# Attention over 32 images: the two half-empty key tiles of an image pair become one, and GpSimd pre-adds twelve tiles instead of nine

## The reference, cut to what matters

```python
g = clip(bn1(conv1x1(l)), 0, 6)                  # 64 channels
f = einsum('niab,nicd->nabcd', theta, theta)     # theta = first 32 channels
f = softmax(f.reshape(n, h*w, h, w), axis=1)     # over the first pixel index
f = softmax(f.reshape(n, h*w, h*w), axis=2)      # over the second pixel index
out = einsum('nabcd,nicd->niab', f, g) / h * w
out = bn2(depthwise_conv3x3(out)) + l
```

## Time and profile before

| | |
|---|---|
| median of three runs | 5523.3 us (5523.17 to 5526.93) |
| the profiled execution | 5524.6 us |
| its span | 5522.8 us |
| granted TensorE clock, mean | 0.988 |
| frames | 32, after 790 us of layer 0 |

### The profile page before, as it was taken

How to read it: one execution, slowest core, us unless ns; L and a number is a source line. 1 busy time by engine, 2 the same in 40 slices (tenths; PEclk the granted TensorE clock), 3 DMA queues, 4 the chain that set the end, 5 groups by cost and what they waited for, 6 DMA issues and landing times.

```text
span 5522.8 us, 92847 instructions
## 1 busy us (share of the span) xinstructions
PE 5347.5 (97%) x34434; PEld 2656.0 (48%) x34434; DVE 4534.5 (82%) x9093; ACT 5218.8 (94%) x3077; POOL 3992.9 (72%) x1715
## 2 busy tenths in 40 slices
PE   8999969999999999999999999999999999999996
PEld 3444434455454444444444444555544444444442
DVE  7888867888888888888888888888888888888886
ACT  7888859999999999999999999999999999999995
POOL 5666624878777777777777777887877777777775
PEclk9999979999999999999999999999999999999998
DMA  7778851222222222222222222222222222222211
GB/s 148 164 160 161 162 101 33 56 48 46 60 60 60 60 60 60 60 60 60 59 54 59 57 54 50 57 55 48 49 60 60 60 60 60 60 60 60 60 37 36
DMA packets 225087, 382.64 MB, mean 69 GB/s; under 512 B 155837, under 2 KB 173438, under 8 KB 214398
## 3 DMA queue, kind: packets, MB, share of 16 engines
q1 hardware_dynamic: 224638, 376.69, 32.8%
HBM read 260.16 MB, written 103.56 MB: 66 GB/s over the span
## 4 chain that ended last, share of the span: by engine, by line
PE 79%; issue 3%; DVE 2%; ACT 1%; DMA 0%; SPq 0%; POOL 0%; DVEq 0%; POOLq 0%
PE at_AV L924 40%; PE at_S L894 23%; PE at_AV L929 14%; PE at_AV L920 2%; DVE at_ring L803 1%; ACT at_ring L748 1%; ACT at_ring L754 1%; DVE at_OUTB L834 0%; DMA at_YT<-yd 0%; DVE at_RZ L820 0%; DMA rzd<-at_ZC 0%; DMA at_ZB<-rzd 0%; SPq L648 0%; SPq L612 0%; DVE at_CIN L830 0%
## 5 line engine op out<-in xcount | busy, mean ns | idle before, releaser
L803 DVE TENSOR_SCALAR_CACHE_REDUCE at_ring<-at_S 128x1176 f32<-128x1176 f32 (+1 forms) x2400 | 2952.7, 1242 | 323.8 <-PE at_S L894 296.5
L748 ACT ACTIVATE at_ring<-at_ring,at_NM 128x3136 f32<-128x3136 f32 (+1 forms) x800 | 2324.4, 2905 | 102.5 <-DVE at_NM L812 98.8
L712 POOL TENSOR_TENSOR at_ZP<-at_ZP,at_ring 128x1568 f32<-128x1568 f32 x512 | 1827.8, 3609 | 747.3 <-ACT at_ring L754 719.9
L924 PE MATMUL at_AV<-at_ring,at_GT 128*64 128x392 f32 x12800 | 2316.3, 501 | 8.9 <-issue 8.9
L754 ACT ACTIVATE at_ring<-at_ring,at_RZ 128x3136 f32<-128x3136 f32 (+1 forms) x800 | 2319.8, 2900 | 0.0
L894 PE MATMUL at_S<-at_THM,at_THS 128*128 128x392 f32 x6400 | 1512.2, 365 | 96.1 <-DVE at_ring L803 52.7
L894 PEld LDWEIGHTS at_S<-at_THM,at_THS 128*128 128x128 f32 x6400 | 1058.8, 187 | 799.8 <-DVE at_ring L803 505.0
L924 PEld LDWEIGHTS at_AV<-at_ring,at_GT 128*64 128x64 f32 x12800 | 837.5, 136 | 1146.5 <-issue 1109.1
L725 POOL TENSOR_TENSOR at_OUTB<-at_OUTB,at_ZB 128x1568 f32<-128x1568 f32 x248 | 887.2, 3578 | 18.1
L929 PE MATMUL at_AV<-at_ring,at_ones 128*32 128x392 f32 x8192 | 756.8, 498 | 0.0
L858 DVE TENSOR_TENSOR at_ACC<-at_AV,at_ACC 128x392 f32<-128x392 f32 x768 | 433.4, 564 | 257.2 <-PE at_AV L924 253.2
(11 more groups left out here) (64 smaller groups left out, 2385.8 us busy)
## 6 DMA issues: line engine op xcount, KB each, us to landing
l_X<-in_x SPq DMA_DIRECT2D x128, 392.0 KB, 7.4
at_THM<-hld SPq DMA_DIRECT2D x128, 392.0 KB, 8.3
at_CIN<-att SPq DMA_DIRECT2D x64, 406.0 KB, 7.6
at_ZB<-rzd SPq DMA_DIRECT2D x64, 406.0 KB, 4.9
at_THS<-hld SPq DMA_DIRECT2D x128, 200.0 KB, 4.9
yd<-l_YO SPq DMA_DIRECT2D x128, 196.0 KB, 5.5
att<-at_ACC SPq DMA_DIRECT2D x256, 98.0 KB
at_OUTB<-yd SPq DMA_DIRECT2D x64, 392.0 KB, 8.8
```

What stands on the lines that cost most here:

```text
L712: e.tensor_tensor(z, z, v, ALU.add).then_inc(g_add, 1)
L748: e.activation(v, v, ACT.Exp, bias=NM[0:k, i:i + 1], accum_out=ZS[0:k, i:i + 1]).then_inc(a_p1, 1)
L803: e.tensor_scalar(ring[0:r, s % RING, QC * a_:QC * b].rearrange("p (b w) -> p b w", w=QC), PS[0:r, k % 2, 0:b - a_, 0:QC], 1.0, None, ALU. ...
L924: ins = e.matmul(dst[64 * j:64 * j + 64, 0:QC], GT[fl.n % 2][0:r, t, :], ring[0:r, slot, q:q + QC], start=(t == GROUPS[fl.i][0]), stop=(t ...
```

## The change

- The 64 keys that are left over of image 2p and those of image 2p+1 share one tile: a pair of images takes 49 slots (`PAIR`) instead of 50. Image 2p has slots 0 to 24, image 2p+1 slots 24 to 48; slot 24 is the shared one, the last tile of the first image and the first (t = 0) of the second. `THL` holds the 64 keys of each image in its own half of 128 columns, zeros in the other half; for the shared slot each block of 392 columns takes two matmuls (one per image) that accumulate. `GT` and `ones` have zeros in the other image's half.
- `POOL_OF` becomes (2, 2, 2, 2, 2, 2, 0); in group 0 tiles 1 and 2 are taken, so the pooled tiles are 1, 2, 4, 5, 8, 9, 12, 13, 16, 17, 19, 20.
- The costs that `plan` uses for ScalarE change from 2910 and 2900 to 2810 and 2893 ns; shared score pieces cost double.
- SyncE gets the loads `thl`; the due slots of `thm`, `ths` follow the new numbering. Six more memsets stand ahead of the attention.

```diff
-KEYS = [128] * 24 + [64]
+HALF_KEYS = 24
+PAIR = 2 * NT - 1
-POOL_OF = (1, 2, 2, 2, 1, 1, 0)
-POOLED = [t for r, m in zip(GROUPS, POOL_OF) for t in r[:m]]
+POOL_OF = (2, 2, 2, 2, 2, 2, 0)
+POOLED = [t for g, (r, m) in enumerate(zip(GROUPS, POOL_OF)) for t in (r[:m] if g else r[1:1 + m])]
+def base(n):
+    return PAIR * (n // 2) + (NT - 1) * (n % 2)
+def keys_of(n, t):
+    return t if n % 2 == 0 else t - 1 if t else HALF_KEYS
+def tiles_of(s):
+    p, r = divmod(s, PAIR)
+    return ([(2 * p, r)] if r < NT else []) + ([(2 * p + 1, r - NT + 1)] if r >= NT - 1 else [])
...
-    total = NT * n_img
+    total = PAIR * n_img // 2
...
-            ta = t_a + (2910 if n_a % 2 or n_a == 0 else 2900)
+            ta = t_a + (2810 if n_a % 2 or n_a == 0 else 2893)
...
+                tp = t_s + 178 * (b - a) * len(tiles_of(n_s // NP)) + turn
...
-        THS = sb("THS", [128, HW], F32R)
+        THS = sb("THS", [128, 2 * HALF], F32R)
+        THL = sb("THL", [128, 2, 128], F32R)
...
+            def thl(n):
+                if n >= 2:
+                    e.wait_ge(pe_s, NP * (PAIR * (n // 2 - 1) + NT))
+                i = n % 2
+                for blk in range(4):
+                    e.dma_start(THL[32 * blk:32 * blk + 32, i, 64 * i:64 * i + 64].bitcast(F32),
+                                hld[n, blk // 2, :, 2 * HALF:]).then_inc(s_thl, 16)
...
-                todo.append((f - NT + 0.2 if n >= 1 else -9, thm, (n,)))
-                todo.append((f - NT + 13 if n >= 1 else -8, ths, (n, 0)))
-                todo.append((f + 0.1 if n >= 1 else -7, ths, (n, 1)))
+                todo.append((f - NT + 1.2 if n >= 1 else -9, thm, (n,)))
+                todo.append((f - NT + 14 if n >= 1 else -8, ths, (n, 0)))
+                todo.append((f - NT + 15 if n >= 2 else -6.5, thl, (n,)))
+                todo.append((f + 1.1 if n >= 1 else -7, ths, (n, 1)))
...
                 for j in range(a_, b):
-                    ins = e.matmul(PS[0:r, k % 2, j - a_, 0:QC], THS[:, 128 * t:128 * t + r],
-                                   THM[n % 2][:, QC * j:QC * j + QC], start=True, stop=True)
+                    for i, (n, t) in enumerate(of):
+                        q = 128 * keys_of(n, t)
+                        own = THS[:, q:q + 128] if len(of) == 1 else THL[:, i, :]
+                        ins = e.matmul(PS[:, k % 2, j - a_, 0:QC], own, THM[n % 2][:, QC * j:QC * j + QC],
+                                       start=(i == 0), stop=(i == len(of) - 1))
```

More of the change, by code:

```diff
@@ L71, in plan @@
         for b, r in enumerate(BATCHES):
-            f = NT * (n - 1) + 8 + 4 * b
+            f = base(n) - NT + 8 + 4 * b
             pre.append(Fill("g", n, b, 0, f if n else -1, f + 3 if n else -1))
         for g, r in enumerate(GROUPS):
-            first = NT * n + r[-1]
+            first = base(n) + r[-1]
             main += [Fill("o", n, g, p, first, 0) for p in range(4)]
             main += [Fill("z", n, g, i, first, 0) for i in range(2)]
-    adds = [(NT * n + t, h) for n in range(n_img) for t in POOLED for h in range(2)]
+    adds = [(n, t, h) for n in range(n_img) for t in POOLED for h in range(2)]
     conv = [(n, step) for n in range(n_img - 1) for step in range(20)]
@@ L138, in plan @@
             if s >= RING:
[L139 to L142, removed]
+                for m, u in tiles_of(s - RING):
+                    free = max(free, group_end.get((m, group_of(u)), inf) + LAT)
+                    if u in POOLED:
+                        free = max(free, end_add.get((m, u, 1), inf) + LAT)
             cv.append((max(td, end_s.get(n_m, inf) + LAT, free), 2, "M"))
@@ L154, in plan @@
         if adds:
-            s, h = adds[0]
-            n, t = divmod(s, NT)
+            n, t, h = adds[0]
             free = -inf
@@ L159, in plan @@
                 free = summed.get((n - 1, h), inf) + LAT
-            cg.append((max(tg, end_p2.get(s, inf) + LAT, free), 0, "add"))
+            cg.append((max(tg, end_p2.get(base(n) + t, inf) + LAT, free), 0, "add"))
         if conv:
@@ L228, in plan @@
             if what == "add":
-                s, h = adds.pop(0)
-                n, t_ = divmod(s, NT)
+                n, t_, h = adds.pop(0)
                 tg = end_add[n, t_, h] = t + (1700 if t_ == POOLED[0] else 3600)
-                pool.append(("add", s, h))
+                pool.append(("add", (n, t_), h))
             else:
@@ L543, in attention @@
         RZ = sb("RZ", [128, 4])
-        ones = sb("ones", [128, 32])
+        ones = sb("ones", [128, 3, 32])
         WG = sb("WG", [65, C])
@@ L607, in ths @@
             def ths(n, h):
-                lo, hi = (0, HALF) if h == 0 else (HALF, HW)
+                lo, hi = (0, HALF) if h == 0 else (HALF, 2 * HALF)
                 if n >= 1:
-                    e.wait_ge(pe_s, NP * (NT * (n - 1) + (12 if h == 0 else NT)))
+                    e.wait_ge(pe_s, NP * (base(n - 1) + (n - 1) % 2 + (12 if h == 0 else 24)))
                 for blk in range(4):
@@ L686, in _ @@
         def _(e):
-            for t in (ones,):
-                e.memset(t[:, :], 1.0).then_inc(g_ms, 1)
+            e.memset(ones[:, 0, :], 1.0).then_inc(g_ms, 1)
+            e.memset(ones[:, 1:3, :], 0.0).then_inc(g_ms, 1)
+            e.wait_ge(g_ms, 2)
+            for i in range(2):
+                used, rest = (slice(64 * i, 64 * i + 64), slice(64 - 64 * i, 128 - 64 * i))
+                e.memset(ones[used, 1 + i, :], 1.0).then_inc(g_ms, 1)
+                e.memset(GT[i][rest, HALF_KEYS, :], 0.0).then_inc(g_ms, 1)
+                e.wait_ge(g_ms, 4 + 2 * i)
+            e.memset(THL[:, :, :].bitcast(F32), 0.0).then_inc(g_ms, 1)
             e.memset(CIN[:, :, :], 0.0).then_inc(g_ms, 1)
@@ L699, in _, with add @@
             T3 = ZB[:, 1:29, :]
-            def add(s, h):
-                n, t = divmod(s, NT)
+            def add(n, t, h):
+                s = base(n) + t
                 v = ring[:, s % RING, HW // 2 * h:HW // 2 * (h + 1)]
@@ L731, in _ @@
                 if what == "add":
-                    add(n, i)
+                    add(*n, i)
                 else:
@@ L844, in evacuate @@
                     r = BATCHES[fl.i]
-                    full = [t for t in r if KEYS[t] == 128]
-                    spans = [(128, full[0], len(full))] + [(KEYS[t], t, 1) for t in r if KEYS[t] != 128]
+                    full = [t for t in r if t != HALF_KEYS]
+                    h = 64 * (fl.n % 2)
+                    spans = [(slice(0, 128), full[0], len(full))] + [(slice(h, h + 64), HALF_KEYS, 1)] * (HALF_KEYS in r)
                     for p, t0, m in spans:
                         o = t0 - r[0]
-                        v = src[0:p, 64 * o:64 * (o + m)].rearrange("p (t c) -> p t c", c=64)
-                        ins = e.tensor_scalar(GT[fl.n % 2][0:p, t0:t0 + m, :], v, 0.0, 6.0, ALU.max, ALU.min)
+                        v = src[p, 64 * o:64 * (o + m)].rearrange("p (t c) -> p t c", c=64)
+                        ins = e.tensor_scalar(GT[fl.n % 2][p, t0:t0 + m, :], v, 0.0, 6.0, ALU.max, ALU.min)
                 elif fl.kind == "o":
@@ L882, in scores @@
                 s, c = divmod(k, NP)
[L883 to L889, removed]
+                of = tiles_of(s)
+                for n, t in of:
+                    if t == 0 and c == 0:
+                        e.wait_ge(s_thm[n % 2], 64 * (n // 2 + 1))
+                    if keys_of(n, t) in (0, 12) and c == 0:
+                        e.wait_ge(s_ths[keys_of(n, t) // 12], 64 * (n + 1))
+                if len(of) == 2 and c == 0:
+                    e.wait_ge(s_thl, 128 * (of[0][0] // 2 + 1))
                 if k >= 2:
@@ L913, in unit @@
                     else:
-                        e.wait_ge(a_p2, NT * fl.n + GROUPS[fl.i][-1] + 1)
+                        e.wait_ge(a_p2, base(fl.n) + GROUPS[fl.i][-1] + 1)
                         e.wait_ge(v_ev, index["g", fl.n, 3, 0] + 1)
-                o = t - BATCHES[fl.i][0] if fl.kind == "g" else 0
-                slot = (NT * fl.n + t) % RING
+                slot = (base(fl.n) + t) % RING
+                part = 0 if t == SUM or keys_of(fl.n, t) != HALF_KEYS else 1 + fl.n % 2
                 for _, j in fl.units[i]:
                     if fl.kind == "g":
-                        ins = e.matmul(dst[0:r, 64 * o:64 * o + 64], YT[(4 * fl.n + fl.i) % 2][:, 128 * o:128 * o + r],
+                        o = t - BATCHES[fl.i][0]
+                        a_, b = (128 * o, 128 * o + 128) if t != HALF_KEYS else (128 * o - 64 * (fl.n % 2), 128 * o + 64)
+                        ins = e.matmul(dst[0:b - a_, 64 * o:64 * o + 64], YT[(4 * fl.n + fl.i) % 2][:, a_:b],
                                        WG[:, :], start=True, stop=True)
@@ L923, in unit @@
                         q = QC * (2 * fl.j + j)
-                        ins = e.matmul(dst[64 * j:64 * j + 64, 0:QC], GT[fl.n % 2][0:r, t, :], ring[0:r, slot, q:q + QC],
```

(6 more changed lines are left out.)

49 lines of the change are left out of this document (24 added, 25 removed).

## The result

The changed kernel takes 5719.7 us (median of four runs, 5712.66 to 5723.8) against 5523.7: a ratio of 1.035, 95% interval 1.033 to 1.037. It is 196 us slower; I had forecast 92.

The account below looks back on a forecast made before the run. TensorE bounds by a small margin, ScalarE next. Frame 139.4 + 1.3 + 7.0 + 1.3 = 149.0 us against 145.8; thirty such frames +96, two others -10, start and tail +2: +88, giving 5615 us, range 5395 to 5760.

Parts of the forecast that it names:

- parts 1 and 2: Per frame, ScalarE needs 139.4 us (2.9 less) and TensorE 140.0 (4.2 less); with 1.3 of ScalarE waiting, 140.7.
- uncoupled frame: Frame without VectorE waiting for late stores: 140.7 us, 5.1 less than before.
- Start and tail: Six memsets and four small loads at the start, plus the tail: +2 us, bounds 0 and 5.
- coupling: VectorE's copy into ACC waits for stores behind the late convolution; ScalarE stands still 7.0 us, clock adds 1.3 per frame.
- part 3: GpSimd gets 21.4 us more additions per frame; its convolution ends about 26 us into the next frame instead of 1.1.
- part 4: SyncE's queue behind the convolution: 15.5 us until stores land, at 41.5 into the frame, wanted at about 33.2.
- The wait: VectorE waits 8.3 us per frame for the landed stores before group 0's copy into ACC; ScalarE stands still 7.0.
- The clock: TensorE's clock falls behind a gap of 4 us or more: 1.3 us per frame, bounds 0 and twice that.
- Uncoupled: Rival: convolution ends before 17.5 us or the store stands later; TensorE and ScalarE just get faster, 5363 us; chance 0.14.
- The case of a last step behind the additions of tile 2: Rival: GpSimd's convolution ends at 34 us; 5735 if in every second frame, 5855 in all; chance 0.15.

Follow-up runs that it names:

- late_store: Changed kernel with only the output store moved in SyncE's order, behind the stores of ACC and ZACC: 5451.3 us, ratio 0.987 to the kernel before.
- warm: Kernel with the late output store plus ten unused filler matmuls in TensorE's gaps in every even frame from image 2 on: 5425.2 us, ratio 0.982.
- Shared_only: Changed kernel with the old number of pooled tiles, so the shared tile alone: 5473.9 us, ratio 0.991 to the kernel before.
- late_store_b: Kernel with the late output store run once more, without fillers, on the same chip as the kernel with fillers: 5445.4 us.
- thm_last: Changed kernel with only the load of THM moved, behind the ACC stores and the convolution's loads: 5567.1 us.

## Why the prediction was right in its mechanism and short by half

- **Engines (parts 1 and 2): the failed step.** "Of the 3.5 us that ScalarE waits now I leave 1.3" gave an uncoupled frame of 140.7. Late_store, where no copy L890 waits for the stores, shows (140.1 + 146.6) / 2 = 143.3: ScalarE waits 3.9, not 1.3. That is 2.6 more per frame, 80 us of the 105 that the forecast lacked. The windows of an odd and an even frame of late_store show most of it:

```profile
2658.50:2805.00 146.50, 145.36 (x912) 74.75 (x908) 122.54 (x251) 143.51 (x76) 134.21 (x46) 1.00 0.30 63
2805.00:2945.10 140.10, 136.30 (x842) 71.56 (x842) 115.36 (x238) 137.54 (x72) 130.32 (x44) 0.98 0.25 52
```

TensorE's average, 140.8, is near my 140.0, but its work isn't spread evenly: 434 of the L963 records fall in an odd frame and 366 in an even one (400 in each frame before), as the order of the fills has it. So TensorE, busy 145.4 of 146.5, bounds the odd frame, and ScalarE with 24 x 5.69 = 136.6 the even one. I took the larger of two averages, where the time is the average of two larger values. Over the engine that bounds it each kind of frame takes about the 1.3 that I had: 146.6 for 145.4, and 137.9 for 136.6 as long as the clock holds (warm). But in even frames the relieved TensorE loses its clock for 6.8 us, which costs 2.2. ScalarE's 142.3 leaves 4.3 us of an odd frame. Shared_only agrees: TensorE is busy 148.3 of 148.4 in its odd frames, and the even ones take 139.5. So going from nine to twelve pooled tiles shortens the odd frames alone and is worth 22 us (5473.9 to 5451.3), where 4.2 us off every frame would be 134. The 4.2 itself is a little low: a unit of the z products takes 3.12 / 4 = 0.78 us, not 0.70, which makes 4.7; the forecast doesn't hang on it.
- **Start and tail.** Forecast +2; the attention starts 2.0 later, but from the first exponential of the last image to the end it takes 233.1 us instead of 207.8. Of these 25 us, 18 are the coupling in this last, odd frame (late_store: 215.0) and 7 are there without it.
- **GpSimd (part 3).** Right in kind: the convolution ends 18.0 and 31.0 us into the frames, 24.5 on average, for a forecast of 26. Even and odd frames differ by 13 us, which I had averaged away. I had also left its start at 50.4 us; it is 58.1 in even and 71.2 in odd frames, since its loads stand behind the late stores in SyncE's order. The average hides a threshold: with the end at 18.0 an even frame takes 140.0 us, no more than in late_store (140.1), and with the end at 31.0 an odd one takes 17.5 more.
- **SyncE (part 4).** Forecast 15.5 us from the convolution's end to the landed stores, measured 20.5. The landing was taken as 0.9 us from a moment with an empty queue; behind 1.6 MB of `THM` it is 4.6, and the issues of `THM` took 2.5 instead of 1.8.
- **The wait.** 8.3 us of VectorE per frame forecast; measured about 17.2 in odd frames and 1.1 to 2.4 in the even ones from image 4 to 28, where the frame is no longer for it. With the clock, the coupling costs (164.1 - 146.6) / 2 = 8.75 per frame, for a forecast of 7.0 + 1.3 = 8.3. Two errors offset each other here: a chain 5 us too short and an end 1.5 us too late on average, against frames that don't pay.
- **The clock.** 1.3 us was taken for each coupled frame, and none for the uncoupled ones; the half-clock stretches of the changed kernel are 6.8 us in nearly every even frame and mostly 17.1 in an odd one. Of the latter only 3.7 to 6.9 lie behind TensorE's gap, the rest within it. What they cost apart from the gap no run shows.
- **The rivals.** Uncoupled isn't this kernel, and its 5363 was 88 us under late_store, where the coupling is gone, and 62 under the fastest kernel tried. The case of a last step behind the additions of tile 2 didn't come: the last step stands behind the copies of tile 1 [L742 above], as forecast. The end at 31 goes with the late start of the convolution: 7.7 us later than 50.4.

## What to carry to other kernels

Before work is added to an engine with idle time, ask what waits for that engine in an in-order queue, and what is issued behind that wait. Here a store that nobody needed soon sat ahead of stores that gated the next image; its place cost 268 us, and moving it was worth more than either half of the change. Where two kinds of frame alternate, work out which engine bounds each kind; averages over both gave 140.7 here for 143.3. When the engine that bounds is relieved, look at what its new gaps do to its clock before counting the gain.

## What the runs showed of the hardware

- Two gaps of TensorE of 0.6 and 1.2 us close together were followed by a stretch at half clock in 15 of the 16 even frames of late_store, 6.8 us in thirteen of them; a third gap, of 0.4 us in those thirteen, lies within the stretch. The single gap of 1.1 us in the kernel before was followed by one in one frame of thirty, and in late_store_b one even frame had the gaps and kept its clock. With ten filler matmuls in the gaps none of the fifteen even frames that had them showed a slow stretch. Useless work made the kernel 20 us faster on the same chip.
- Eight stores of 1.6 KB had landed 0.9 us after their last issue in thm_last, and 4.6 us after it in the changed kernel, where four loads of 392 KB had been issued 8 us before.
